# A new first stage for a transformer block: strips first, a second head group's strips, wide q stores, unread products in the waits

## The chip, the cores and the metric

The kernel runs on one core of one Trainium2 chip. The metric is the device time of one execution in microseconds (us). Engine names are those of the profile: PE is TensorE (its matmuls), PEld its weight loads, DVE is VectorE, ACT is ScalarE, POOL is GpSimd, SP is SyncE. SPq and ACTq are the DMA issues of SP and ACT.

## The reference

An adaLN transformer block on x of 8 batches, 512 tokens and 128 channels, cut here to what matters:

```python
mod = (silu(c) @ wmod).reshape(8, 6, 1, 128)       # sa, ca, ga, sb, cb, gb
h = layernorm(x) * (1 + ca) + sa
q, k, v = heads(h @ bin(Wq).T + bq), ...           # 16 heads of 8; bin(W) = sign(W) * mean|W| of a row
x = x + ga * (softmax(q @ k.T * 8**-0.5) @ v @ bin(Wp).T + bp)
h = layernorm(x) * (1 + cb) + sb
x = x + gb * (shared_ffn(h) + top2_of_8_experts(h))
```

## The kernel before

Attention comes first, batch by batch (B0 to B7), then a mixture of experts in units of rows. In attention a batch has 16 slots. A slot n takes one head group (four heads, `n // 4`) and one quarter of the keys: four score products (`scores`, L1609), four exponentials on ACT (L868), and one slot later the products with v (`products`, L1620). An exponential needs the row's maximum. It is found ahead of time in "fills": `max_scores` makes q·k for one head and half of the queries into a bank of 1,024 columns (L1594), and `maxima` reduces it on DVE (L1077). There are 32 fills to a batch, eight to a head group. Steady slots have two fills. Slots 0 to 4 of B0 have three (`CATCH_UP`), as they begin with 11 fills (`FIRST_FILLS`) made ahead of them.

Scores are made of bf16 parts: q and k are split in three (`first_part` on DVE, then `split_qk`), stored to DRAM (`store_q_heads`, the k stores of ACT), and read back as stacks of 72 rows (`load_q_stack`, `load_k_stack`). The stack's last two rows are the negated maxima: after eight fills, `max_T` transposes them, `split_max` splits them on DVE, and a DMA lays them in (`m_row_loaded`). This trip is long, so the fills of B0's head group 0 (`DIRECT_FILLS`, 8) don't use the stacks: `project_direct` (L1646) projects the same heads a second time in f32, each head in a strip of 32 partitions, and `max_scores` multiplies the strips directly (L1584), four matmul instructions a fill. DVE reduces these at L1074.

The first stage is thus, by engine and in program order:

- SP: loads x, the four weights, bq, bk, bv, bp, router bias, three shared matrices, then x of B1 once B0's layer norm is done; stores q's parts in six DMAs (head group 0, then the rest), loads x of B2, then the q stacks of groups 0 and 1, waits for group 1's stack and the row maxima (L523), and loads groups 2 and 3.
- DVE: layer norm of B0, weight cleaning (`clean_weights`, twice), statistics of B1, q's first part and whole split, layer norm of B1, k's first part, fills 0 to 7, `split_max`, fills 8 to 10.
- PE: c and router transposes, modulation, `ln1_T(B0)`, `spread_bias` (biases into the strips; waits for all five small loads), `weights_T(0)`, `project` q, `project_direct` k and q, `project` k, fills 0 to 10 with `weights_T(2)`, `project_v`, `ln1_T(B1)`, `project` q of B1 and `max_T` between them, `project` k of B1, then slot 0.
- ACT: evacuates each of these in PE's order; stores and loads k's parts of groups 0 and 1.
- POOL: constants, reciprocal deviations (`rstd`), k's split.

`misc` is one PSUM bank that all transposes and projections share, in the order of the list `BEFORE`; each waits until the one before is evacuated.

Of the kernel before, what the change touches and what calls it, by code (L numbers as in the profile page):

```python
# [5 lines left out]
ALU = mybir.AluOpType  # L6
# [5 lines left out]
P = 128  # L12
B, T, C = 8, 512, 128
H = 16
DH = C // H
TT = T // P
HG = 4
# [20 lines left out]
DIRECT = 1  # L38
DIRECT_FILLS = DIRECT * 2 * HG
# [14 lines left out]
def adaln_block(nc: bass.Bass, x, Wq, bq, Wk, bk, Wv, bv, Wp, bp, sh_gate, sh_up, sh_down,  # L54
                gate_w, up_w, down_w, router_w, routing_bias, c, wmod, out):
    ctx = ExitStack()
    with ctx:
# [26 lines left out]
        w_sgn = scratch[0][:, 0:4 * C].rearrange("p (i c) -> p i c", c=C)  # L84
        w_neg = scratch[0][:, 4 * C:8 * C].rearrange("p (i c) -> p i c", c=C)
# [128 lines left out]
        first_stored = [sem(f"first_stored{i}") for i in range(2)]  # L214
        small_loaded = sem("small_loaded")
        c_loaded = sem("c_loaded")
# [85 lines left out]
        BEFORE = ["c", "mod", "ln1_0", "q_0", "k_0", "v_0", "ln1_1", "q_1", "m0", "k_1"]  # L302
# [119 lines left out]
        def first_part(dve, b, i, done):  # L422

            if b.const > 0:
                dve.wait_ge((q_stored, k_stored)[i], all_stored(b.plus(-1), i))
            if b.const == 1:
                dve.wait_ge(first_stored[i], 16 * (PARTS, 1)[i])
            dve.wait_ge(misc_free, done + 1)
            dve.tensor_copy(qk_parts[i][:, 0, :], qk_f[i][:]).then_inc(first_ready, 1)  # L429
# [13 lines left out]
        def load_k_stack(eng, b, g):  # L443

            eng.wait_ge(*((first_stored[1], 16) if b.const == 0 and g == 0 else (k_stored, all_stored(b, 1))))
# [37 lines left out]
        def _(sp):  # L483
            sp.dma_start(x_in[:], x[0].rearrange("(p t) c -> p t c", p=P)).then_inc(x_in_loaded, 16)
            for i, w in enumerate((Wq, Wk, Wv, Wp)):
                sp.dma_start(w_nat[:, i, :], w).then_inc(w_loaded[i // 2], 16)
            for i, v in enumerate((bq, bk, bv)):
                sp.dma_start(bias_qkv[:, i:i + 1], v.rearrange("(p o) -> p o", o=1)).then_inc(small_loaded, 16)
# [5 lines left out]

            def load_x(b):

                sp.wait_ge(ln1_ready, TT * b.n)
                sp.dma_start(x_in[:], x[bass.ds(b.n, 1)].rearrange("o (p t) c -> p (o t) c", p=P)).then_inc(x_in_loaded, 16)
# [19 lines left out]
            def load_q_stack(b, g):  # L518
# [3 lines left out]
                if b.const > 0 or g > 0:  # L522
                    sp.wait_ge(q_stored, all_stored(b, 0))  # L523
# [54 lines left out]
            for i in range(2):  # L578
                store_parts(B1, i)
# [94 lines left out]
        def _(pool):  # L674
# [11 lines left out]
            def rstd(mv, ve, ve_ready, out_, ready, stats_ready, b):  # L686
# [8 lines left out]
            pool.affine_select(out=earlier_token[:], in_=ones_bf[:], compare_op=ALU.is_gt, fill=0.0, base=0,  # L695
                               pattern=[[1, P]], channel_multiplier=-1).then_inc(consts_ready, 1)
            pool.memset(marks[:], 0.0).then_inc(consts_ready, 1)

            pool.sem_inc(rows_free, 2)
            pool.iota(expert_no[:], pattern=[[1, E]], base=0, channel_multiplier=0,  # L700
                      allow_small_or_imprecise_dtypes=True).then_inc(consts_ready, 1)
            pool.iota(next_row[0][:], pattern=[[REGION, E]], base=0, channel_multiplier=0,
                      allow_small_or_imprecise_dtypes=True).then_inc(consts_ready, 1)
            for k in range(RING):
                pool.memset(digit[:, k:k + 1], float(E ** k)).then_inc(consts_ready, 1)
            pool.memset(pad_rows[:], 0.0).then_inc(pad_ready, 1)
            pool.wait_ge(pad_ready, 1)
            pool.memset(pad_rows[:, :, C + 1], float(FAR)).then_inc(pad_ready, 1)
            pool.iota(first_row[:], pattern=[[REGION, E]], base=0, channel_multiplier=0,
                      allow_small_or_imprecise_dtypes=True).then_inc(consts_ready, 1)  # L710
            pool.iota(unit_start[:], pattern=[[P, 2 * EARLY_PAIRS]], base=0, channel_multiplier=0,
                      allow_small_or_imprecise_dtypes=True).then_inc(consts_ready, 1)
            pool.affine_select(out=earlier[:], in_=ones_bf[:, 0:E * E].rearrange("p (e f) -> p e f", e=E), compare_op=ALU.is_gt,
                               fill=0.0, base=0, pattern=[[1, E], [-1, E]], channel_multiplier=0).then_inc(consts_ready, 1)
            pool.iota(home[:], pattern=[[TOKENS, K_TOP], [1, TT]], base=0, channel_multiplier=TT,
                      allow_small_or_imprecise_dtypes=True).then_inc(setup_pool, 1)
# [53 lines left out]

            pool.wait_ge(setup_pool, 4)
            rstd(mv1, ve1, var1_ready, rstd1, rstd1_ready, stats1_ready, B1)
            split_qk(pool, B0, 1)
# [51 lines left out]
        def _(act):  # L825
# [91 lines left out]
            for h0, h1, stored in ((0, HG, first_stored[1]), (HG, H, k_stored)):  # L917
                act.dma_start(k_dram[0][h0:h1].rearrange("h d i t -> (h d) i t"), qk_parts[1][DH * h0:DH * h1]).then_inc(stored, 16)
# [102 lines left out]
        def _(dve):  # L1021
# [251 lines left out]

            dve.memset(strip_rows[:], 0.0).then_inc(strips_ready, 1)
# [208 lines left out]
        def _(pe):  # L1483
# [10 lines left out]

            pe.wait_ge(consts_ready, 2)
            pe.wait_ge(c_loaded, 32)
            pe.transpose(misc[:, 0:B], c_nat[:], ident[0:B, 0:B])
            pe.transpose(misc[:, B:B + E], router_nat[:], ident[0:E, 0:E]).then_inc(misc_full, 1)
            free(use(AHEAD, "mod"))
# [72 lines left out]
            def max_scores(b, g, hh, half):  # L1572
# [3 lines left out]
                if fill < DIRECT_FILLS:  # L1576
                    g, pair, t = direct_fill(fill)
                    if fill % (2 * HG) == 0:
                        pe.wait_ge(first_done, (4,)[g])
# [300 lines left out]
```

## Time and profile before

| | |
|---|---|
| median of 3 runs | 668.17 us (664.99 to 668.57) |
| the profiled execution | 667.02 us, its span 665.2 us |
| mean granted TensorE clock | 0.977 |
| PE busy | 615.2 us, 92% |
| DVE busy | 504.9 us, 76% |
| ACT busy | 404.1 us, 61% |

The span runs from the first to the last instruction. Busy shares are averages over stages with different limits. The granted clock is given as a share of 2.4 GHz, so 0.5 is the lower level of 1.2 GHz. The first stage is the first 37 us; slots 0 to 4 of B0 follow, up to 60.6 us.

### The profile page before, as it was taken

To read this page: it belongs to the slowest core of one execution; us is meant where nothing else is said; L and a number is where in the kernel's file an instruction comes from. 1 tells how busy PE (TensorE), PEld (TensorE's weight loads), DVE (VectorE), ACT (ScalarE), POOL (GpSimd) and SP (SyncE) were. 2 spreads that over 40 slices of the span, in tenths; PEclk is the share of its full clock that TensorE was granted. 3 is DMA by queue.
4 is the path that set the end of the run, shared out by engine and by line. 5 is a ranking of instruction groups with operands and counts; after the bars stand their busy time and mean duration, and the time that the engine had idled before them with its cause. 6 is when DMAs were issued, how large, how long until landed. Compare 5 with 4: busy or idle time off the path is not lost.

```text
span 665.2 us, 10688 instructions
## 1 busy us (share of the span) xinstructions
PE 615.2 (92%) x3461; PEld 288.7 (43%) x3461; DVE 504.9 (76%) x1065; ACT 404.1 (61%) x791; POOL 259.2 (39%) x309
## 2 busy tenths in 40 slices
PE   4899999999999999999999999999999589886997
PEld 2332324233333333423333333232378578776855
DVE  5779788889988989888998888988467534433567
ACT  2345777777777776777778778678735224433431
POOL 4240041414352451434336235025056656566610
PEclk9969999999999999999999999999999988997999
DMA  3443332442541445344244244214832223222155
GB/s 103 134 121 117 117 114 98 132 131 90 160 123 64 133 134 134 109 149 116 93 147 127 69 133 130 67 50 135 226 81 57 68 65 88 63 68 61 56 185 195
DMA packets 58828, 73.91 MB, mean 111 GB/s; under 512 B 10857, under 2 KB 39819, under 8 KB 58772
## 3 DMA queue, kind: packets, MB, share of 16 engines
q1 hardware_dynamic: 53144, 63.30, 32.0%
q0 software_dynamic: 4320, 8.47, 3.7%
q10 hardware_dynamic: 1308, 1.46, 0.8%
q8 instruction: 28, 0.46, 0.3%
q14 instruction: 28, 0.23, 0.1%
HBM read 38.36 MB, written 34.96 MB: 110 GB/s over the span
## 4 chain that ended last, share of the span: by engine, by line
PE 73%; DVE 12%; ACT 7%; issue 3%; another core or an unknown queue 2%; DMA 1%; SPq 1%; POOL 1%; ACTq 1%; DVEq 0%; POOLq 0%
PE pv L1620 15%; PE st L1609 15%; PE mx L1594 14%; PE mx L1806 7%; DVE neg_max L1077 6%; PE st L1820 5%; PE mx L1754 3%; PE misc L1487 2%; PE misc L1514 2%; PE st L1770 2%; ACT pt L868 2%; PE pv L1794 1%; PE misc L1520 1%; DVE stats_sb L1026 1%
## 5 line engine op out<-in xcount | busy, mean ns | idle before, releaser
L868 ACT ACTIVATE pt<-st 128x512 f32<-128x512 f32 x496 | 282.1, 598 | 105.8 <-PE st L1609 95.9
L1077 DVE TENSOR_REDUCE neg_max<-mx 128x2 f32<-128x1024 f32 x248 | 294.5, 1215 | 47.9 <-PE mx L1594 44.6
L1620 PE MATMUL pv<-pt,vs 128*32 128x512 f32 x1024 | 136.4, 605 | 0.3 <-ACT pt L868 0.3
L745 POOL DMA_INDIRECT routed<-rec,row_u x64 | 64.1, 1002 | 136.6 <-PE pv L1620 114.8
L812 POOL DMA_INDIRECT results<-qs,home_u x71 | 72.0, 1014 | 50.8 <-ACT qs L995 28.4
L1609 PE MATMUL st<-even_qk 74*128 74x512 bf16 x256 | 89.0, 389 | 1.9 <-ACT pt L868 1.1
L1609 PE MATMUL st<-qs,ks 74*128 74x512 bf16 x240 | 81.4, 383 | 1.8 <-ACT pt L868 1.1
L1594 PE MATMUL mx<-ks,qs 72*128 72x512 bf16 x256 | 76.5, 380 | 2.9 <-DVE neg_max L1077 2.5
L1594 PE MATMUL mx<-even_qk 72*128 72x512 bf16 x240 | 74.5, 393 | 4.4 <-DVE neg_max L1077 4.1
L437 POOL TENSOR_TENSOR qk_r<-qk_f,qk_parts 128x512 f32<-128x512 f32 x15 | 17.4, 1161 | 98.8 <-DVE qk_parts L429 98.7
L1609 PEld LDWEIGHTS st<-even_qk 74*128 74x128 bf16 x256 | 20.9, 99 | 71.5 <-ACT pt L868 51.7
L989 ACT ACTIVATE vs<-mx 128x512 f32<-128x512 f32 (+1 forms) x43 | 22.7, 527 | 43.8 <-PE mx L1806 20.9
L1609 PEld LDWEIGHTS st<-qs,ks 74*128 74x128 bf16 x240 | 18.8, 98 | 67.5 <-ACT pt L868 51.5
L1806 PE MATMUL mx<-vs,pt 128*128 128x256 f32 (+1 forms) x224 | 48.1, 361 | 0.0
L1370 DVE TENSOR_TENSOR vs<-vs,mx 128x512 f32<-128x512 f32 (+1 forms) x29 | 17.2, 591 | 36.8 <-ACT vs L989 34.4
L1620 PEld LDWEIGHTS pv<-pt,vs 128*32 128x32 f32 x1024 | 20.1, 108 | 52.9 <-issue 37.6
L995 ACT ACTIVATE qs<-st,ks 128x128 f32<-128x128 f32 x71 | 23.2, 370 | 32.2 <-PE st L1820 20.6
L1806 PEld LDWEIGHTS mx<-vs,pt 128*128 128x128 f32 x224 | 38.8, 208 | 3.4
L1594 PEld LDWEIGHTS mx<-even_qk 72*128 72x128 bf16 x240 | 22.2, 100 | 35.0 <-DVE neg_max L1077 13.0
L1594 PEld LDWEIGHTS mx<-ks,qs 72*128 72x128 bf16 x256 | 23.7, 98 | 31.4 <-DVE neg_max L1077 8.2
L1794 PE MATMUL pv<-ident,ks 128*128 128x128 f32 x71 | 15.7, 287 | 21.9 <-ACT vs L984 13.4
L1370 DVE TENSOR_TENSOR pt<-vs,mx 128x512 f32<-128x512 f32 (+1 forms) x14 | 8.3, 591 | 24.0 <-issue 23.5
(217 smaller groups left out, 798.0 us busy)
## 6 DMA issues: line engine op xcount, KB each, us to landing
routed<-pad_rows SPq DMA_DIRECT2D x64, 260.0 KB
even_qk<-q_parts SPq DMA_DIRECT2D x48, 96.0 KB
qs<-q_parts SPq DMA_DIRECT2D x48, 96.0 KB
ks<-k_parts SPq DMA_DIRECT2D x48, 96.0 KB
even_qk<-k_parts SPq DMA_DIRECT2D x42, 96.0 KB
ks<-routed SPq DMA_DIRECT2D x28, 130.0 KB
q_parts<-qk_parts SPq DMA_DIRECT2D x21, 128.0 KB
k_parts<-qk_parts SPq DMA_DIRECT2D x7, 384.0 KB, 2.3
```

The costliest lines, as they stand in the source:

```text
L745: pool.indirect_dma_start(out=routed_dram, out_offset=bass.IndirectOffsetOnAxis(ap=row_u[:, k, t:t + 1], axis=0), in_=rec[b.par][:, k, t, ...
L812: pool.indirect_dma_start(out=result_dram, out_offset=bass.IndirectOffsetOnAxis(ap=home_u[:, slot, h:h + 1], axis=0), in_=y_u[slot][:, h, ...
L868: act.activation(pt[n % 2][:, hh, :], score_bank(b, n, hh), ACT.Exp, scale=SCALE).then_inc(exp_done, 1)
L989: act.activation(silu_u[u % 2][:, 0:halves(u) * I], up_bank(u, 0), ACT.Silu).then_inc(silu_ready, 1)
L995: last = act.activation(y_u[u % RING][:, h, :], y_bank(u)[:, h, :], ACT.Copy, scale=xu[u % RING][:, h, C:C + 1])
L1077: dve.tensor_reduce(neg_max[g % 2][:, hh, 2 * half:2 * half + 2], mx_bank[half][:], AX_X, ALU.max, negate=True).then_inc(mx_free, 1)
L1370: dve.tensor_tensor(act_u[u % ARING][:, 0:halves(u) * I], silu_u[u % 2][:, 0:halves(u) * I], up_bank(u, 1), ALU.mult).then_inc(act_ready, 1)
L1594: last = pe.matmul(mx_bank[half][:, t, :], qs[b.par][0:PROD, h, q0:q0 + P], ks[b.par][0:PROD, h, :], start=True, stop=True)
L1609: pe.matmul(score_bank(b, n, hh), ks[b.par][0:STACK, h, j * P:(j + 1) * P], qs[b.par][0:STACK, h, :], start=True, stop=True).then_inc(st_f ...
L1620: last = pe.matmul(pv_bank[32 * hh:32 * (hh + 1), :], vs[b.par][:, j, HG * g + hh, :], pt[n % 2][:, hh, :], start=(n % Y_SLOTS == 0), stop ...
L1806: last = pe.matmul(up_bank(u, m // IC)[:, m % IC * rows:(m % IC + 1) * rows], w_unit[u % WRING][:, m * P:(m + 1) * P], xuT[u % 2][:, 0:row ...
L1820: last = pe.matmul(y_bank(u)[:, h, :], act_u[u % ARING][:, first:first + P], w_unit[u % WRING][:, 2 * I + j * C:2 * I + (j + 1) * C], star ...
```

## The change

The strips of head group 1 are made too, and the fills that use strips become twelve (all of the 11 made ahead, and the first of slot 0). Strips are projected ahead of q itself. `spread_bias` waits for bq and bk alone, which are loaded right after Wq and Wk. q's parts are split on POOL, stored in three DMAs of all heads, and the stacks are loaded group by group. `max_T` of group 0 comes ahead of `ln1_T(B1)`. `keep_busy` puts matmuls into PE's waits whose products nobody reads: bf16, 128x128 by 128x512, into a free bank. In all there are 33 of them: 7, 5, 4, 2 and 2 ahead of the first projection, 1, 1, 1, 1, 4 and 1 between the fills, and 3 ahead of slot 0; and a DVE memset makes their operand.

```diff
-DIRECT = 1
-DIRECT_FILLS = DIRECT * 2 * HG
+DIRECT = 2
+DIRECT_FILLS = 3 * HG
...
-        BEFORE = ["c", "mod", "ln1_0", "q_0", "k_0", "v_0", "ln1_1", "q_1", "m0", "k_1"]
+        BEFORE = ["c", "mod", "ln1_0", "q_0", "k_0", "v_0", "m0", "ln1_1", "q_1", "k_1"]
...
@@ sync
-            for i, w in enumerate((Wq, Wk, Wv, Wp)):
-                sp.dma_start(w_nat[:, i, :], w).then_inc(w_loaded[i // 2], 16)
-            for i, v in enumerate((bq, bk, bv)):
-                sp.dma_start(bias_qkv[:, i:i + 1], v.rearrange("(p o) -> p o", o=1)).then_inc(small_loaded, 16)
+            for i, w in enumerate((Wq, Wk)):
+                sp.dma_start(w_nat[:, i, :], w).then_inc(w_loaded[0], 16)
+            for i, v in enumerate((bq, bk)):
+                sp.dma_start(bias_qkv[:, i:i + 1], v.rearrange("(p o) -> p o", o=1)).then_inc(qk_bias_loaded, 16)
+            for i, w in enumerate((Wv, Wp)):
+                sp.dma_start(w_nat[:, 2 + i, :], w).then_inc(w_loaded[1], 16)
...
+            load_x(B1)
+            sp.dma_start(bias_qkv[:, 2:3], bv.rearrange("(p o) -> p o", o=1)).then_inc(small_loaded, 16)
...
-            load_x(B1)
             sp.wait_ge(parts_ready, 1)
-            store_q_heads(0, HG, first_stored[0])
-            store_q_heads(HG, H, q_stored)
-            load_x(B1.plus(1))
-            sp.wait_ge(first_stored[0], 16 * PARTS)
+            store_q_heads(0, H, q_stored)
             load_q_stack(B0, 0)
-            load_q_stack(B0, 1)
-            sp.wait_ge(stack_loaded[0][1], STACK_DMAS)
-            sp.wait_ge(m_row_loaded[0], ROW_DMAS)
-            for g in (2, 3):
+            for g in (1, 2, 3):
                 load_stack(B0, g)
+                if g == 2:
+                    load_x(B1.plus(1))
...
@@ gpsimd
+            split_qk(pool, B0, 0)
+            split_qk(pool, B0, 1)
+            rstd(mv1, ve1, var1_ready, rstd1, rstd1_ready, stats1_ready, B1)
             pool.affine_select(out=earlier_token[:], in_=ones_bf[:], compare_op=ALU.is_gt, fill=0.0, base=0,
...
             pool.wait_ge(setup_pool, 4)
-            rstd(mv1, ve1, var1_ready, rstd1, rstd1_ready, stats1_ready, B1)
-            split_qk(pool, B0, 1)
             fill_values(pool, 1)
...
@@ scalar
-            act.wait_ge(setup_pool, 3)
-            for i in range(2):
-                load_ones(act, i)
...
             evacuate_wT(0, 2)
-            act.wait_ge(small_loaded, 80)
-            evacuate_qk(B0, 0, use(AHEAD, "q_0"))
             act.wait_ge(first_done, 1)
             evacuate_direct(1, 0, 3)
             evacuate_direct(0, 0, 4)
+            evacuate_qk(B0, 0, use(AHEAD, "q_0"))
             evacuate_qk(B0, 1, use(AHEAD, "k_0"))
+            act.wait_ge(setup_pool, 3)
+            load_ones(act, 0)
             evacuate_wT(2, 5)
             act.activation(exp_first[:], strip_rows[:], ACT.Exp)
-            act.wait_ge(parts_ready, 2)
...
             act.wait_ge(v_ready[0], 2)
             evacuate_v(B0, use(AHEAD, "v_0"))
+            act.wait_ge(parts_ready, 2)
+            for h0, h1, stored in ((0, HG, first_stored), (HG, H, k_stored)):
+                act.dma_start(k_dram[0][h0:h1].rearrange("h d i t -> (h d) i t"), qk_parts[1][DH * h0:DH * h1]).then_inc(stored, 16)
+            evacuate_direct(1, 1, 6)
+            evacuate_direct(0, 1, 7)
             act.wait_ge(key_ones[0], 16)
             load_k_stack(act, B0, 0)
-            load_k_stack(act, B0, 1)
-            project_in(B1, use(AHEAD, "ln1_1"))
-            evacuate_qk(B1, 0, use(AHEAD, "q_1"))
+            act.wait_ge(small_loaded, 48)
             act.wait_ge(misc_free, use(AHEAD, "m0") + 1)
             for k in range(M_PARTS):
                 act.dma_start(qs[0][MROW + k:MROW + k + 1, 0:HG, :].rearrange("p h (t q) -> p (h t) q", t=TT),
                               m_rows[0][:, k, :]).then_inc(m_row_loaded[0], 16)
+            project_in(B1, use(AHEAD, "ln1_1"))
+            evacuate_qk(B1, 0, use(AHEAD, "q_1"))
+            load_ones(act, 1)
...
@@ vector
             first_part(dve, B0, 0, use(AHEAD, "q_0"))
-            split_qk(dve, B0, 0)
+            maxima(range(1))
+            first_part(dve, B0, 1, use(AHEAD, "k_0"))
+
+            maxima(range(1, 2 * HG))
             layer_norm1(B1)
-            first_part(dve, B0, 1, use(AHEAD, "k_0"))
-
-            maxima(range(DIRECT_FILLS))
             split_max(B0, 0, use(AHEAD, "m0"))
-            maxima(range(DIRECT_FILLS, FIRST_FILLS))
+            maxima(range(2 * HG, FIRST_FILLS))
...
@@ tensor
+            def keep_busy(count, into):
+
+                ones = busy_ops.bitcast(BF16)
+                for _ in range(count):
+                    pe.matmul(into, ones[:, 0:P], ones, start=True, stop=True)
...
-                pe.wait_ge(small_loaded, 80)
+                pe.wait_ge(qk_bias_loaded, 32)
...
+            keep_busy(4, nothing)
             ln1_T(B0, use(AHEAD, "ln1_0"))
             spread_bias()
+            keep_busy(2, nothing)
             weights_T(0)
-            pe.wait_ge(first_done, 2)
+            keep_busy(2, nothing)
+            free(use(AHEAD, "q_0"))
+            project_direct(1, 0, 2)
+            project_direct(0, 0, 2)
             project(0, use(AHEAD, "q_0"))
-            project_direct(1, 0, 1)
-            project_direct(0, 0, 2)
-            project(1, use(AHEAD, "k_0"))
...
             for fill in range(FIRST_FILLS):
                 max_scores(*fill_of(fill))
+                if fill == 0:
+                    project(1, use(AHEAD, "k_0"))
                 if fill == 1:
+                    keep_busy(1, pv_bank[:])
                     weights_T(2)
+                if fill == 2:
+                    keep_busy(1, pv_bank[:])
                 if fill == 3:
                     pe.wait_ge(first_done, 5)
                     project_v(use(AHEAD, "v_0"))
+                if fill == 4:
+                    keep_busy(1, st_bank[0][:])
                 if fill == 5:
+                    project_direct(1, 1, 4)
+                    project_direct(0, 1, 4)
+                if fill == 6:
+                    keep_busy(1, st_bank[0][:])
+                if fill == 2 * HG - 1:
+                    keep_busy(4, st_bank[0][:])
+                    max_T(B0, 0, use(AHEAD, "m0"))
+                if fill == 2 * HG:
                     ln1_T(B1, use(AHEAD, "ln1_1"))
-                if fill == DIRECT_FILLS - 1:
+                if fill == 2 * HG + 1:
+                    keep_busy(1, st_bank[0][:])
                     project(0, use(AHEAD, "q_1"))
-                    max_T(B0, 0, use(AHEAD, "m0"))
             project(1, use(AHEAD, "k_1"))
+            keep_busy(3, st_bank[0][:])
```

## Rows read from the trace of the kernel before

**Rows 1.** The page: span, and granted clock in 40 slices (tenths).

```profile
span 665.2 us, 10688 instructions
...
PEclk9969999999999999999999999999999988997999
```

**Rows 2.** The chain of waits by time: start us, us, what.

```profile
7.59 2.81 DMA router_bias<-L_ffn_routing_bias
...
60.51 3.40 DVE neg_max L1077 x3
...
72.69 0.86 PE misc L1514 x2
73.77 0.43 PE mx L1594 x2
```

**Rows 3.** Stretches: us, then busy of PE, PEld, DVE, ACT, POOL; clock; DMA share; GB/s.

```profile
10.00:15.00 5.00, 4.08 (x20) 1.39 (x24) 2.80 (x15) 1.49 (x4) 0.58 (x2) 1.00 0.38 115
...
35.00:40.00 5.00, 5.00 (x11) 1.72 (x10) 2.81 (x3) 1.88 (x4) 0.00 (x0) 0.50 0.28 80
...
66.00:200.00 134.00, 130.99 (x747) 45.97 (x746) 115.64 (x197) 100.22 (x183) 42.64 (x50) 1.00 0.40 120
```

**Rows 4.** Single microseconds: the same columns, around the clock's fall.

```profile
29.00:30.00 1.00, 0.00 (x0) 0.00 (x0) 1.00 (x2) 0.68 (x1) 0.00 (x0) 1.00 0.71 206
...
31.00:32.00 1.00, 0.38 (x1) 0.00 (x0) 0.00 (x0) 0.58 (x1) 0.00 (x0) 0.52 0.23 58
```

**Rows 5.** Timeline, up to 18 us: start us, us, engine, line, instructions [idle before].

```profile
6.37 1.68 DVE L1034 TENSOR_SCALAR ln<-x_in,mv,rstd 128x128 f32<-128x128 f32 x4 [1.58 <-POOL rstd L691]
...
8.19 1.09 PE L1487 MATMUL misc<-ident,ln 128*128 128x128 f32 x4 [1.11 <-DVE ln L1034]
...
9.24 0.48 DVE L1052 TENSOR_SCALAR w_nat<-pt,alpha 128x128 f32<-128x128 f32 x2
...
9.38 0.78 ACT L845 ACTIVATE hT<-misc,mod_T 128x512 f32<-128x512 f32 x1 [2.02 <-PE misc L1487]
...
10.66 0.69 PE L1628 MATMUL st<-ident,w_nat 128*128 128x128 f32 x2
...
11.39 0.38 ACT L893 ACTIVATE wT<-st 128x256 f32<-128x256 f32 x1 [0.33 <-PE st L1628]
...
13.83 1.94 PE L1646 MATMUL st<-hT,wT 128*32 128x512 f32 x8
...
14.00 0.69 ACT L853 ACTIVATE qk_f<-misc,bias_qkv 128x512 f32<-128x512 f32 x1 [2.23 <-PE misc L1514]
```

**Rows 6.** Timeline from 18 us to slot 0: the same columns.

```profile
18.46 1.99 PE L1584 MATMUL mx<-x 32*128 32x512 f32 x8
...
19.63 4.81 DVE L1074 TENSOR_REDUCE neg_max<-mx 128x2 f32<-128x1024 f32 x4
19.79 1.15 POOL L437 TENSOR_TENSOR qk_r<-qk_f,qk_parts 128x512 f32<-128x512 f32 x1 [4.10 <-DVE qk_parts L429]
...
25.69 3.58 ACTq L448 DMA_DIRECT2D even_qk<-k_parts  x6
...
33.20 1.24 ACTq L928 DMA_DIRECT2D even_qk<-m_rows  x2
```

**Rows 7.** Timeline from slot 0 on: the same columns.

```profile
37.40 1.06 PE L1609 MATMUL st<-even_qk 74*128 74x512 bf16 x2
...
39.35 1.22 DVE L1077 TENSOR_REDUCE neg_max<-mx 128x2 f32<-128x1024 f32 x1 [2.19 <-PE mx L1594]
...
45.10 1.22 DVE L1077 TENSOR_REDUCE neg_max<-mx 128x2 f32<-128x1024 f32 x1 [1.59 <-PE mx L1594]
...
51.34 1.07 PE L1620 MATMUL pv<-pt,vs 128*32 128x512 f32 x8
...
69.25 0.60 PE L1487 MATMUL misc<-ident,ln 128*128 128x128 f32 x4
```

**Rows 8.** DMA issues by line: KB each, us from issue to landing.

```profile
k_parts<-qk_parts ACTq DMA_DIRECT2D x1, 96.0 KB, 2.6
```

More of the change, by code:

```diff
@@ L84, in adaln_block @@
         w_sgn = scratch[0][:, 0:4 * C].rearrange("p (i c) -> p i c", c=C)
+        busy_ops = scratch[1][:, 0:T // 2]
         w_neg = scratch[0][:, 4 * C:8 * C].rearrange("p (i c) -> p i c", c=C)
@@ L213, in adaln_block @@
         strips_ready = sem("strips_ready")
-        first_stored = [sem(f"first_stored{i}") for i in range(2)]
+        busy_ready = sem("busy_ready")
+        first_stored = sem("first_stored")
         small_loaded = sem("small_loaded")
+        qk_bias_loaded = sem("qk_bias_loaded")
         c_loaded = sem("c_loaded")
@@ L425, in first_part @@
                 dve.wait_ge((q_stored, k_stored)[i], all_stored(b.plus(-1), i))
-            if b.const == 1:
-                dve.wait_ge(first_stored[i], 16 * (PARTS, 1)[i])
+            if b.const == 1 and i == 1:
+                dve.wait_ge(first_stored, 16)
             dve.wait_ge(misc_free, done + 1)
@@ L443, in load_k_stack @@
         def load_k_stack(eng, b, g):
-            eng.wait_ge(*((first_stored[1], 16) if b.const == 0 and g == 0 else (k_stored, all_stored(b, 1))))
+            eng.wait_ge(*((first_stored, 16) if b.const == 0 and g == 0 else (k_stored, all_stored(b, 1))))
             for j in range(PARTS):
@@ L694, in _ @@
             rstd(mv1, ve1, var1_ready, rstd1, rstd1_ready, stats1_ready, B0)
[L695 to L716, printed above, removed]
             def residual(b):
@@ L769, in scatter @@
                     scatter_rows(b, i)
+            split_qk(pool, B0, 0)
+            split_qk(pool, B0, 1)
+            rstd(mv1, ve1, var1_ready, rstd1, rstd1_ready, stats1_ready, B1)
+            pool.affine_select(out=earlier_token[:], in_=ones_bf[:], compare_op=ALU.is_gt, fill=0.0, base=0,
+                               pattern=[[1, P]], channel_multiplier=-1).then_inc(consts_ready, 1)
+            pool.memset(marks[:], 0.0).then_inc(consts_ready, 1)
+            pool.sem_inc(rows_free, 2)
+            pool.iota(expert_no[:], pattern=[[1, E]], base=0, channel_multiplier=0,
+                      allow_small_or_imprecise_dtypes=True).then_inc(consts_ready, 1)
+            pool.iota(next_row[0][:], pattern=[[REGION, E]], base=0, channel_multiplier=0,
+                      allow_small_or_imprecise_dtypes=True).then_inc(consts_ready, 1)
+            for k in range(RING):
+                pool.memset(digit[:, k:k + 1], float(E ** k)).then_inc(consts_ready, 1)
+            pool.memset(pad_rows[:], 0.0).then_inc(pad_ready, 1)
+            pool.wait_ge(pad_ready, 1)
+            pool.memset(pad_rows[:, :, C + 1], float(FAR)).then_inc(pad_ready, 1)
+            pool.iota(first_row[:], pattern=[[REGION, E]], base=0, channel_multiplier=0,
+                      allow_small_or_imprecise_dtypes=True).then_inc(consts_ready, 1)
+            pool.iota(unit_start[:], pattern=[[P, 2 * EARLY_PAIRS]], base=0, channel_multiplier=0,
+                      allow_small_or_imprecise_dtypes=True).then_inc(consts_ready, 1)
+            pool.affine_select(out=earlier[:], in_=ones_bf[:, 0:E * E].rearrange("p (e f) -> p e f", e=E), compare_op=ALU.is_gt,
+                               fill=0.0, base=0, pattern=[[1, E], [-1, E]], channel_multiplier=0).then_inc(consts_ready, 1)
+            pool.iota(home[:], pattern=[[TOKENS, K_TOP], [1, TT]], base=0, channel_multiplier=TT,
+                      allow_small_or_imprecise_dtypes=True).then_inc(setup_pool, 1)
             pool.wait_ge(setup_pool, 4)
-            rstd(mv1, ve1, var1_ready, rstd1, rstd1_ready, stats1_ready, B1)
-            split_qk(pool, B0, 1)
             fill_values(pool, 1)
@@ L1272, in late_tables @@
                     unit_experts(EARLY_PAIRS, TABLE - EARLY_PAIRS, tables_ready)
+            dve.memset(busy_ops, 1.0).then_inc(busy_ready, 1)
             dve.memset(strip_rows[:], 0.0).then_inc(strips_ready, 1)
@@ L1492, in free @@
                 pe.wait_ge(misc_free, done)
+            def keep_busy(count, into):
+                ones = busy_ops.bitcast(BF16)
+                for _ in range(count):
+                    pe.matmul(into, ones[:, 0:P], ones, start=True, stop=True)
+            nothing = mx_bank[1][:, 1, :]
+            pe.wait_ge(busy_ready, 1)
+            keep_busy(7, nothing)
             pe.wait_ge(consts_ready, 2)
@@ L1498, in _ @@
             pe.transpose(misc[:, B:B + E], router_nat[:], ident[0:E, 0:E]).then_inc(misc_full, 1)
+            keep_busy(5, nothing)
             free(use(AHEAD, "mod"))
@@ L1587, in max_scores @@
                     return
-                if hh == 0 and half == 0:
+                if hh == 0 and half == 0 or fill == DIRECT_FILLS:
                     pe.wait_ge(stack_loaded[b.par][g], STACK_DMAS * (b.half + 1))
```

13 lines of the change are left out of this document (5 added, 8 removed).

## The prediction

> **What bounds the kernel now.** I read the page first. Its span is 665.2 us, and of the 40 slices the third is the only one of the attention part in which PE's granted clock is clearly down [rows 1]. The windows come next, as they say what bounds each stage: from 66 to 200 us PE is busy 131 of 134 us, DVE 116, ACT 100 [rows 3]. So attention from slot 6 on is bound by PE, and the change touches nothing there. What the change can give is a shift: the time at which the first slots of B0 are done. I look for one event that fixes it and take the end of fill 26, the last of three reductions that the chain of waits shows from 60.51 to 63.91 [rows 2]. From there to 200 us the program is the same and its order too.
>
> Before that event there are three stretches. Up to 18.5 us the strips and projections are made. In this stretch the windows print a clock of 1.00 [rows 3], but the durations contradict it: eight instructions of strip projection take 1.94 us, and the same shape takes 1.07 at 51.34 [rows 5, 7]. I take it that PE ran at its lower level and that the record has no entry until the clock changes. From 18.5 to 37.4 DVE and PE take turns, DVE reduces fills 0 to 7 in some 10.6 us from 19.63 [rows 6], then everything waits for stacks and row maxima. The clock is recorded as falling to the lower level at 31 us, behind a microsecond with no PE work [rows 4], and is still there at 40 [rows 3]. From 37.4 on slots 0 to 4 run, and there DVE decides: three reductions to a slot at 1.13 to 1.2 us each [rows 2], with idle time of 2.19 and 1.59 ahead of fills 11 and 14 [rows 7].
>
> **The change, part by part.** Full-level prices: 0.86 us for a projection, 0.43 for two bf16 products of 512 columns, so 0.215 for one [rows 2]; 1.0 for four strip projections (1.07 as busy time [rows 7]); 0.95 for a strip fill, half of 1.99 for eight instructions [rows 6]; 0.60 for four transposes [rows 7]. A reduction takes 1.21 [rows 6].
>
> *Start to fill 0.* B0's layer norm ends at 8.05 as before [rows 5]; nothing of the change is ahead of it but a memset on DVE and the order of loads behind x. If the first 16 unread products have brought the clock up, transposes take 0.60 for 1.09, and hT (0.78) is ready near 9.55. `spread_bias` no longer waits for the router bias, which landed at 10.4 [rows 2]. The cleaned weights are there at 9.72 [rows 5], their transposes and copy (0.69 halved, 0.38) end near 10.5, and the two pairs of unread products (4 x 0.215) fit into the waits. The first projection starts at 10.5, not 11.8 (the copy ends at 11.77 [rows 5]). k strips, q strips and q follow: 1.0 + 1.0 + 0.86, to 13.35. ACT copies the q strips by 13.35, fill 0 starts at 13.4 for 18.46 [rows 6]. ACT then has q at 14.1 (0.69 [rows 5]), DVE its first part at 14.6, and reduces fill 0 from there: 5.0 us ahead of 19.63 [rows 6].
>
> *Fills 0 to 7.* PE now has more to do here: project k after fill 0, the strips of group 1 after fill 5 (2.0 us), eight unread products. DVE does k's first part (0.43), but no split. Followed in order, with a fill waiting for the reduction two before it: reductions of fills 1, 2, 3 run back to back from 16.5 to 20.1; fill 4 is late behind `project_v` (as many columns as a projection, 0.86) by 0.6; fill 6 is late behind the strips by 1.8 (PE 21.9 to 23.9, then the fill to 24.8). The last reduction ends at 27.3. That is 12.7 us for eight fills, where before it was 10.6, and gives back 2.1 of the 5.0.
>
> *To slot 0.* Before, nothing reduced from 30.2 to 33.6, as fill 8 needed group 1's stack and DVE waited for `max_T`. Now `max_T` runs at 27.4 (its four unread products, 0.86, end at 26.8 and cost nothing), B1's layer norm takes DVE to 28.4, `split_max` to 28.95. ACT issues the row maxima to 30.2 (1.24 [rows 6]), which puts hT of B1 behind them, to 31.0. PE: fill 8, transposes of B1, fill 9 and one unread product by 30.6, a wait of 0.45, project q to 31.9, fill 10 to 32.85, project k to 33.7 (ACT frees the bank at 32.7), three unread products to 34.35. Here the 0.64 us are on the path, as nothing waits there: I book them in full. Slot 0 starts at 34.35 for 37.4 [rows 7], 3.0 earlier.
>
> *Slots 0 to 4.* Fill 11 is now a strip fill: 0.95 for 0.43, so its reduction starts near 35.85, for 39.35 [rows 7]: 3.5 earlier. From there the DVE work is unchanged. Before it took 63.91 - 39.35 = 24.56 us, of which 1.59 ahead of fill 14 was waiting for PE at the lower level [rows 7]. With PE at its upper level this wait goes, but some 0.5 remains, as PE alternates with DVE in slots 2 and 3. Gain there 1.1. The sum at fill 26 is 3.5 + 1.1 = 4.6 us.
>
> *Transfers.* q's split moves from DVE to POOL, three steps of which the first is 1.15 [rows 6]; I take 3.2 us: parts at 17.8, k's at 21.0, as POOL does one after the other. q's store waits for all heads: three issues to 20, landing after 2.6 to 4 us, by 24 at the latest (the row is of 96 KB [rows 8]). k's store by ACT ends with its first group landed at 24.1 (2.6 [rows 8]), behind it stand the copies of the new strips (to 24.7), then three loads of 0.6 each (3.58 for six [rows 6]), to 26.6. Landed by 29.5 if they take 3 us. Slot 0 needs them at 34.35: 4.8 us of cover. Groups 1 to 3 are loaded by SP from 24 on at about 3.7 us each; group 1 is needed only by fill 12, no longer by fill 8. B2's x moves behind group 2 and is needed in slot 1. POOL's constants move behind the splits and feed nothing before slot 0 except the v values of B1, which end near 27. All of these I cost at nothing, with that cover.
>
> *Where a page speaks against it.* Rows 3 and 5 show a recorded 1.00 beside matmuls at half speed. The Trainium skill ("TensorE: Matmul & The Clock Gate", Part 1) says that the lower clock is the default and that activity lifts it; by this rule the trace agrees. The same page (Part 4) says that transposes don't count as activity, which would leave the first rise to the unread products alone. If the rise comes in the first 8 us, the sum stays; if not, it is the first rival.
>
> **Sum.** 667.0 for the profiled execution less 4.6 is 662.4; the same off the median of 668.2 is 663.6. I forecast 663.0. A difference under 0.5% (3.3 us) can't be told from none.
>
> **The rivals.** *The clock is late.* The rises in the trace came only behind long full-width work (13.83 on), and with a gap between the first seven and the next five products it may stay low until after the first projections. Then what I took at full level is at half: 16 unread products take 3.4 us more, of which about 1 stands ahead of `ln1_T` (it would start near 9.1); transposes, weights and four more products add 0.5, 0.35 and 0.4 on the path. The first projection would start near 12.8. Gain 4.6 - 2.3 = 2.3, time 665. For it: nobody can see the clock's phase. Chance 0.14.
>
> *The clock falls all the same before slot 0.* Strip fills use 64 rows, they are most of the work, and before it fell at 31 after them. If it falls near 31, q, fill 10, k and three products take 3.35 more, fill 11 0.95 more, and the 1.1 of slots 0 to 4 is lost: 4.6 - 5.4, time 667.5. Against it: in my walk PE waits at most 0.5 at a time there, where before it had a whole microsecond without work at 29 [rows 4]. Chance 0.1.
>
> *Slower.* It is the same fall, but earlier, behind the strips of group 1 at 24. Then fills 6 to 10 take 0.95 more each (4.75), the projections 1.7, the unread products 1.9, transposes 0.5, fill 11 0.95; less the waits they fill (some 1.5), 8.3 us. It decides from the point at which slot 0 starts later than about 41 (37.4 and 3.3 us more). Slot 0 would start near 41.7 (34.35, and 8.3 less the 0.95 of fill 11), and with the 1.1 lost too the sum is 4.6 - 8.3 - 1.1, 4.8 us later than before: 672. The chance is 0.06: before, 18.5 to 29 held the upper level on just such fills [rows 6].
>
> *The stacks are late.* Slot 0's start is then the landing of k's group 0. It takes 4.8 us more than I think to show, and 8 to lose all. Time 663 to 668, chance 0.05.
>
> *More gain.* The waits of DVE ahead of fills 4 and 6 (0.6 + 1.8) come out half as long, and the 1.59 of slots 0 to 4 is recovered whole: 1.2 + 0.5 on top of 4.6, 6.3 us, time 661 off the profiled execution. Chance 0.12. The forecast itself, 661 to 664.7, keeps 0.53.
>
> **Numbers.** Faster by over 0.5% (under 664.8): forecast, more gain, and less than half of the late clock and late stacks, 0.71. Within 0.5%: the rest of these and the fall at 31, 0.21. Slower: 0.08. The range runs from 659 to 667.6, leaving the slower rival and single runs as far apart as those of before (665.0 to 668.6) outside.
>
> **What would show it.** In the profile after: strip projections of 1.0 to 1.1 us near 10.5; first reduction at L1074 near 14.6, the eighth ending near 27.3; DVE idle of about 1.8 ahead of fill 6; twelve, not eight, reductions at L1074; first scores near 34.4; no 0.5 in the third slice; end of fill 26 near 59.3. The prediction is wrong if PE's clock is at 0.5 between 24 and 45 us, if the first scores wait for a DMA, or if fill 26 is early and the end isn't, which would put the loss behind 60 us.

## The result, and the profile after

Over 20 executions each, the changed kernel takes 665.81 us (663.47 to 667.73) and the one before 668.08 (664.99 to 670.88): ratio 0.9967, interval 0.9953 to 0.9981. It is faster, by 2.3 us, where I had forecast 663.0 and a gain of 4.6 of the profiled execution's 667.0. The time lies in the range that I gave (659 to 667.6), but the gain is less than half of the forecast: 2.3 us of 4.6, or of the 5.1 from 668.08 to 663.0. At 0.33% it is also under the 0.5% that I had drawn as the line to "none", an outcome to which I gave a chance of 0.21 against 0.71 for more. On another chip the changed kernel (run a1) has a ratio of 0.9973 (0.9952 to 0.9994). The ratios leave out executions more than 1.5% above the fastest of their kernel: one in e1, one in e2 and two in e8.

The profiled execution of the changed kernel took 667.73 us, by chance the slowest of its 20, so its span says nothing of the gain. I read the stages instead. The page first, against [rows 1]:

```profile
span 666.0 us, 10815 instructions
...
PEclk9999999999999999999999999999999899998899
```

The third slice is at 9, not 6: the fall of the clock ahead of slot 0 is gone. The chain of waits by time (start us, us, what):

```profile
10.31 1.07 PE st L1661 x8
11.38 0.86 PE pv L1661 x8
12.23 1.06 PE misc L1529 x2
13.29 1.06 PE mx L1599 x4
14.35 1.06 PE misc L1529 x2
15.40 1.06 PE mx L1599 x4
...
17.00 1.06 PE mx L1599 x4
18.06 0.32 PE pv L1504
18.38 1.06 PE mx L1599 x4
19.44 1.09 PE misc L1535 x8
20.53 1.06 PE mx L1599 x4
21.58 0.32 PE st L1504
21.91 1.06 PE mx L1599 x4
22.96 0.99 PE st L1661 x8
23.96 0.86 PE pv L1661 x8
24.82 1.06 PE mx L1599 x4
...
26.20 1.08 PE mx L1599 x4
...
27.30 1.23 DVE neg_max L1078
28.53 1.02 DVE ln L1038 x4
...
29.77 0.29 DVE m_rows L1091
...
57.32 3.40 DVE neg_max L1081 x3
...
69.50 0.86 PE misc L1529 x2
70.58 0.44 PE mx L1609 x2
```

Two things are to be seen. Fill 26 ends at 60.72, for 63.91 [rows 2], 3.2 us earlier and not 4.6; the projection 72.69 in [rows 2] is now at 69.50, the same 3.2. And from 10.31 to 27.28 every piece but 0.16 us ahead of `weights_T(2)` is PE's, without a wait for DVE: the stage is bound by PE, strip fills (`mx`, x4) cost 1.06 each, and so do the projections (`misc`, x2) that stand between them. The pieces of 0.32 are single unread products. The windows of the same stretches as in [rows 3], and one of 134 us beginning 3 us earlier (columns as there):

```profile
10.00:15.00 5.00, 4.87 (x25) 1.39 (x24) 2.92 (x13) 2.41 (x4) 0.45 (x1) 1.00 0.39 93
...
35.00:40.00 5.00, 4.64 (x21) 1.83 (x20) 3.03 (x5) 2.97 (x5) 0.51 (x1) 1.00 0.70 157
63.00:197.00 134.00, 130.78 (x746) 45.99 (x746) 115.64 (x197) 100.19 (x182) 42.68 (x50) 1.00 0.39 120
```

The last is the same work in the same time as before (130.78 for 130.99 of PE). The rows of the timeline that answer to [rows 5 to 7]:

```profile
7.69 0.63 PE L1492 MATMUL misc<-ident,ln 128*128 128x128 f32 x4 [0.26 <-DVE ln L1038]
...
10.31 1.07 PE L1661 MATMUL st<-hT,wT 128*32 128x512 f32 x8
...
14.39 1.23 DVE L1078 TENSOR_REDUCE neg_max<-mx 128x2 f32<-128x1024 f32 x1
...
25.92 1.23 DVE L1078 TENSOR_REDUCE neg_max<-mx 128x2 f32<-128x1024 f32 x1 [1.69 <-PE mx L1599]
...
30.13 1.41 ACTq L929 DMA_DIRECT2D even_qk<-m_rows  x2
...
36.14 0.60 PE L1624 MATMUL st<-even_qk 74*128 74x512 bf16 x2
...
37.84 1.23 DVE L1078 TENSOR_REDUCE neg_max<-mx 128x2 f32<-128x1024 f32 x1 [1.97 <-PE mx L1599]
```

Transposes take 0.63 where they took 1.09, and the first strips 1.07 where they took 1.94: the clock is up before the first transposes at 7.69. The very first unread products, from 1.25 on, still took 3.17 us for seven; the four from 6.40 on took 1.02. Of DMA issues, k's part of head group 0 landed in:

```profile
k_parts<-qk_parts ACTq DMA_DIRECT2D x1, 96.0 KB, 1.8
```

**A landmark.** Single executions of one kernel lie some 5 us apart, so experiments on 1 us need a finer measure. In each profile I take the start of the first copy of a finished half batch to `y_strips` on ACT, in slot 8 of B0 where PE bounds already. The rows give the group of all 16 copies, first and last start. Before, then after:

```profile
L874 ACT ACTIVATE y_strips<-pv x16: 597/597/598, 75.5 to 478.4; 128x512 f32<-128x512 f32 x16
```

```profile
L874 ACT ACTIVATE y_strips<-pv x16: 597/598/600, 72.3 to 475.4; 128x512 f32<-128x512 f32 x16
```

The lead of 3.2 is still 3.0 at the end of attention. The rest, a mixture-of-experts part that the change doesn't touch, took 665.2 - 478.4 = 186.8 in the one profile and 666.0 - 475.4 = 190.6 in the other. Three further profiles with total times near these (b3, b4 and a2 below) have 188.7, 188.4 and 188.6. Thus what the pair of spans seems to lose there is that part's own scatter.

### The profile page after: what moved, and what is told of

It is laid out like the page before. It is cut to its first block, busy times and chain, and to the rows that moved or that the text cites. A ratio compares the mean times of both kernels' runs of the same rounds, so it can differ in the third digit from the quotient of the medians.

```text
span 666.0 us, 10815 instructions
## 1 busy us (share of the span) xinstructions
PE 619.9 (93%) x3523; PEld 289.2 (43%) x3525; DVE 502.2 (75%) x1063; ACT 406.2 (61%) x793; POOL 262.6 (39%) x312
## 4 chain that ended last, share of the span: by engine, by line
PE 71%; DVE 13%; ACT 7%; another core or an unknown queue 4%; issue 3%; DMA 1%; POOL 1%; ACTq 0%; DVEq 0%; POOLq 0%
PE pv L1635 15%; PE st L1624 14%; PE mx L1609 13%; PE mx L1839 7%; DVE neg_max L1081 6%; PE st L1853 4%; PE mx L1787 3%; PE misc L1492 2%; PE misc L1529 2%; PE st L1803 2%; ACT pt L868 2%; PE mx L1599 2%; DVE ln L1038 1%; PE misc L1535 1%
## 5 line engine op out<-in xcount | busy, mean ns | idle before, releaser
L1081 DVE TENSOR_REDUCE neg_max<-mx 128x2 f32<-128x1024 f32 x244 | 289.6, 1216 | 43.6 <-PE mx L1609 40.3
L815 POOL DMA_INDIRECT results<-qs,home_u x71 | 72.1, 1016 | 54.1 <-ACT qs L999 36.8
L1624 PE MATMUL st<-even_qk 74*128 74x512 bf16 x256 | 87.6, 383 | 2.4 <-ACT pt L868 1.5
L1609 PE MATMUL mx<-even_qk 72*128 72x512 bf16 x232 | 69.4, 380 | 4.0 <-DVE neg_max L1081 3.4
L1839 PE MATMUL mx<-vs,pt 128*128 128x256 f32 (+1 forms) x224 | 49.9, 371 | 0.0
```

The costliest lines, as they stand in the source:

```text
L815: pool.indirect_dma_start(out=result_dram, out_offset=bass.IndirectOffsetOnAxis(ap=home_u[:, slot, h:h + 1], axis=0), in_=y_u[slot][:, h, ...
L1081: dve.tensor_reduce(neg_max[g % 2][:, hh, 2 * half:2 * half + 2], mx_bank[half][:], AX_X, ALU.max, negate=True).then_inc(mx_free, 1)
L1609: last = pe.matmul(mx_bank[half][:, t, :], qs[b.par][0:PROD, h, q0:q0 + P], ks[b.par][0:PROD, h, :], start=True, stop=True)
L1624: pe.matmul(score_bank(b, n, hh), ks[b.par][0:STACK, h, j * P:(j + 1) * P], qs[b.par][0:STACK, h, :], start=True, stop=True).then_inc(st_f ...
L1839: last = pe.matmul(up_bank(u, m // IC)[:, m % IC * rows:(m % IC + 1) * rows], w_unit[u % WRING][:, m * P:(m + 1) * P], xuT[u % 2][:, 0:row ...
```

## The experiments

The runs were made on four chips. On three of them (e1 to e9, a1, b1, b2) the part behind attention takes some 25 us less, 641.0 to 641.7 us in all for the kernel before; on the fourth (b3, b4, a2, e10) that kernel takes 668.15 us, as in the result. So only ratios and landmarks go from one to the other. "Before" has landmarks 75.5, 73.2, 75.4, 74.2, 74.4 in five profiles; "changed" has 72.3, 71.9, 72.2.

A count first: the diff has 32 unread products, not 33 (20 ahead of the first projection, 9 between the fills, 3 ahead of slot 0). So e2 takes out 12 and not the 13 that its expectation names, and without the seven of e10 25 are left, not 26.

**e1: no unread products.**

```diff
-                for _ in range(count):
+                for _ in range(0):
                     pe.matmul(into, ones[:, 0:P], ones, start=True, stop=True)
```

> The changed kernel with all 33 unread products taken out (they feed nothing, so the result is the same). I read the traces by a landmark, the start of the first copy into y_strips (75.5 us before, 72.3 after), as it scatters less than the whole time. Theory A, the unread products mostly cost PE time in a stage that PE bounds, and the clock doesn't need them: the landmark at 72 to 73. Theory B, they hold the clock: it comes up only near 17 us and falls again near 31, and the landmark is at 75 or later, most or all of the gain gone.

Ratio to before 1.007 (1.0043 to 1.0096), landmark 79.0, and slower than before by more than the change gains. (Six executions.) Theory A falls. The first strips, which took 1.07, are again at the lower level, and the clock is at 0.5 from 31 to 48 us. Only its rise came sooner than theory B had it: at 14.02 a projection already takes 1.12, not at 17. The timeline and the windows (PE busy, clock, DMA share, GB/s):

```profile
10.51 1.93 PE L1661 MATMUL st<-hT,wT 128*32 128x512 f32 x8 [0.57 <-ACT wT L893]
```

```profile
28.00:30.00 2.00, 0.60 (x3) 1.00 0.79 154
30.00:32.00 2.00, 1.90 (x10) 0.74 0.79 154
```

The new order without the unread products has the f32 strip fills 9 to 11 in the slow stretch, at 2.08 each, where before had bf16 ones; it is worse off than the old.

**e2: the first 20 kept, the 12 from fill 1 on taken out.**

```diff
-                    keep_busy(1, pv_bank[:])
                     weights_T(2)
...
-                    keep_busy(4, st_bank[0][:])
                     max_T(B0, 0, use(AHEAD, "m0"))
...
-            keep_busy(3, st_bank[0][:])
```

> The changed kernel with the first 20 unread products kept and the 13 from fill 1 on taken out. Theory A (what is on PE's path costs 0.22 us each): three ahead of slot 0 and about two between the fills are saved, the landmark moves from 72.3 to 71.2 to 71.7, the clock stays up. Theory B (the clock falls without them, near 31 us): strip fills and projections behind it take twice as long, landmark 74 to 75.5.

Ratio 1.0052 (1.0033 to 1.0072), landmark 76.9: theory B, and more than it expected. The windows (PE, PEld, DVE, ACT, POOL, clock, DMA):

```profile
26.00:28.00 2.00, 0.65 (x3) 0.39 (x5) 2.00 (x6) 0.00 (x0) 0.28 (x3) 1.00 0.81 191
28.00:30.00 2.00, 1.89 (x10) 0.89 (x8) 1.91 (x4) 0.00 (x0) 0.00 (x0) 0.69 0.78 179
30.00:32.00 2.00, 2.00 (x5) 0.50 (x6) 0.05 (x1) 0.78 (x1) 0.00 (x0) 0.50 0.84 200
```

The clock falls behind a stretch in which PE had 0.65 us of work in 2, the wait for DVE's eighth reduction. A strip fill then takes 2.01 in the chain of this run.

**e3: strips for head group 0 alone; e5: the same with 14 unread products ahead of fill 8.**

```diff
-DIRECT = 2
-DIRECT_FILLS = 3 * HG
+DIRECT = 1
+DIRECT_FILLS = 2 * HG
...
-                    project_direct(1, 1, 4)
-                    project_direct(0, 1, 4)
```

```diff
                     max_T(B0, 0, use(AHEAD, "m0"))
+                    keep_busy(14, st_bank[0][:])
```

> The changed kernel with strips for head group 0 alone, so fills 8 to 11 go by the stacks as before. Theory A, that the second group's strips are the term I undersized: 2.0 us of projections after fill 5 and 0.6 us more per fill for four fills go, the landmark moves to 70.5 to 71.8. Rival, the stack of group 1 is late for fill 8 (its last k load is issued at 28.3 us in the trace after): fill 8 starts at 30.5 to 31.5 and not at 28.9, and the landmark is 72.3 to 73.5, so the second group is worth its price.

> The changed kernel with strips for head group 0 alone and 14 more unread products (3.0 us) in the wait ahead of fill 8. The kernel with one group's strips had its landmark at 75.3 us, with the clock at 0.5 from 29 to 40 us. If the second group's strips gain because fill 8 needs no stack, this one stays behind: 74 or more. If they gain only because they keep PE at work in that wait, this one is level with the changed kernel: 72 to 73, and the clock stays at 1.0.

e3: ratio 1.0004 (0.9985 to 1.0023), landmark 75.3, later than both theories had it. Fill 8 starts at 32.07, later than the rival said, and the clock falls in the wait (0.70 in the microsecond from 28, then 0.50). The timeline:

```profile
32.07 1.03 PE L1607 MATMUL mx<-even_qk 72*128 72x512 bf16 x2 [4.92 <-DMA even_qk<-k_parts]
```

e5: the clock stays at 1.0 and the landmark is 72.6, so in the profiles most of what the second group's strips give, 2.7 of 3.2 us (75.3 to 72.6 and to 72.1), is that they fill this wait. But its ratio is 1.0009 (0.9986 to 1.0031), 12 executions between 639.2 and 643.4, where the changed kernel has 0.9973 and one of 12 above 640.05. Two things in the record bear on it. In the profile fill 8 still waits for group 1's stack:

```profile
31.59 0.61 PE L1607 MATMUL mx<-even_qk 72*128 72x512 bf16 x2 [1.42 <-DMA even_qk<-k_parts]
```

And the seven executions with a mean clock of 0.999 or 1.0 have a median of 640.4, while the other five, at 0.994 to 0.997, hold the four slowest (642.4 to 643.4). So the clock probably still falls in some executions, perhaps when the stack lands late; none of those was profiled.

**e4 and e8: the kernel before with unread products.** e4 has the first 20 at the changed kernel's places. e8 adds the early loads of bq and bk, single products behind fills 1, 2, 4 and 6, and groups from fill 7 on:

```diff
                 if fill == DIRECT_FILLS - 1:
+                    keep_busy(5, st_bank[0][:])
                     project(0, use(AHEAD, "q_1"))
+                    keep_busy(3, st_bank[0][:])
                     max_T(B0, 0, use(AHEAD, "m0"))
+                    keep_busy(4, st_bank[0][:])
             project(1, use(AHEAD, "k_1"))
+            keep_busy(3, st_bank[0][:])
```

> The kernel before with the first 20 unread products added at the same places, nothing else changed. Theory A, the early clock rise alone: first projections at 1.1 us instead of 1.9, the k parts 2 to 2.5 us earlier, group 1's stack and fill 8 as much earlier, landmark 73 to 73.5 if the later fall at 31 us stays as it was. Rival, the whole gain of the change is this rise and the absent fall: landmark at 72.5 or less. Second rival, bias load at 10.4 us and the stack transfers hold the stage: landmark 75 or more.

> The kernel before with what the change does to the clock and the first waits alone: bq and bk loaded early, the 20 first unread products, single ones behind fills 1, 2, 4, 6, and 5, 3, 4 and 3 of them in the waits from fill 7 to slot 0. Strips of one head group, order of projections, splits and stores as before. If the clock is the main part of the gain, the clock stays at 1.0 and the landmark is at 71.5 to 73. If the new order and the second group's strips are the main part, the landmark is at 73.5 or later though the clock stays up.

e4: ratio 1.0005 (0.9982 to 1.0028), 640.4 to 648.7; the profiled one is the slowest, landmark 80.7, with the clock at 0.5 from 12 to 15 and from 22 to 49 us. There PE waited from 8.7 to 11.9 for the router bias. The second rival had that wait and a landmark of 75 or more, but none of the three expectations had the clock: in this execution it was up early, and fell early too, behind the wait that was left.

e8: the profile has the clock at 1.0 throughout and the earliest landmark but one, 70.4, earlier than the 71.5 to 73 expected. But its 12 executions make two groups, five at 637.7 to 638.5 with a mean clock of 1.0, and seven at 645.4 to 647.9 with 0.983 to 0.987; ratio 1.0022 (0.9982 to 1.0063) without its two slowest, and over all twelve a median of 645.62 for 641.04. With the clock held, the old order and one group's strips are 1.7 us ahead of the changed kernel's landmark (mean 72.1), though fill 0 starts at 14.55 and not at 13.22. So the new order isn't what gains time by itself. What e8 lacks is a held clock in more than half of its executions. Where the clock falls in those I didn't see.

**e6, e7, e10: fewer unread products.** e6 drops the single ones behind fills 1, 2, 4 and 6, e7 the three ahead of slot 0, e10 all seven.

```diff
                 if fill == 1:
-                    keep_busy(1, pv_bank[:])
                     weights_T(2)
-                if fill == 2:
-                    keep_busy(1, pv_bank[:])
...
             project(1, use(AHEAD, "k_1"))
-            keep_busy(3, st_bank[0][:])
```

> The changed kernel without the four single unread products behind fills 1, 2, 4 and 6; the groups of 4, 1 and 3 behind them stay. In the trace after each of these four takes some 0.3 us of a stretch in which PE is busy without a pause. Theory A (they only cost, the others hold the clock): the landmark moves from 72.1 to 71.0 to 71.6. Theory B (strip fills alone let the clock fall): it falls between 24 and 32 us, landmark 74 or more, time 0.5% over the changed kernel's.

> The changed kernel without the three unread products ahead of slot 0, 0.65 us on the chain that ended last. If they are needed for nothing, the landmark moves from 72.1 to 71.4 to 71.7 and the clock stays up. Rival: the clock falls at the start of slot 0, landmark 73 or more. Third: slots 0 to 4 wait on DVE anyway and the landmark stays.

> The changed kernel without the four single unread products behind fills 1, 2, 4 and 6 and without the three ahead of slot 0. Alone, the four gave 1 us (landmark 71.0) and the three 0.2 to 0.5 (71.7). If what holds the clock are the other 26, the landmark is at 70.4 to 70.8. Rival: with all seven gone the clock falls in some executions, which shows as single times 4 us or more above the rest with a clock under 0.995.

e6: ratio 0.9954 (0.9937 to 0.9970), landmark 71.0. e7: 0.9963 (0.9948 to 0.9978), landmark 71.7. e10, on the chip of b3, b4 and a2: 0.9925 (0.9903 to 0.9947), 662.86 us for 668.15, landmark 70.3; its mean clocks, 0.982 to 0.990, are those of the changed kernel on that chip (0.979 to 0.990), and no execution stands apart from the rest. The seven products only cost; the other 25 hold the clock (20 alone, in e2, did not). e10 beats both kernels. In e6 strip fills stand back to back again, and the timeline shows what that does:

```profile
20.03 1.99 PE L1599 MATMUL mx<-x 32*128 32x512 f32 x8
...
25.95 0.81 PE L1504 MATMUL st<-pt 128*128 128x512 bf16 x3 [0.16 <-issue]
27.48 0.27 PE L1542 MATMUL misc<-ident,neg_max 128*16 128x128 f32 x1 [0.72 <-DVE neg_max L1078]
```

Two fills take 1.99 (1.92 in the chain), where two apart take 1.06 each. And the wait for DVE ahead of `max_T`, in which e2 lost the clock, is here filled with the four products for somewhat more than half (0.81 us seen of them, then 0.72 idle).

**e9: q stored in six DMAs again.**

```diff
-            store_q_heads(0, H, q_stored)
+            store_q_heads(0, HG, first_q)
+            store_q_heads(HG, H, q_stored)
```

> The changed kernel with q stored in six DMAs, the first head group ahead, instead of three wide ones. By my prediction's transfers, which I costed at nothing behind 4.8 us of cover, the landmark stays at 72 to 72.4. Rival: SP issues three more DMAs of 0.75 us ahead of the stack loads, group 0's or the later stacks are late, landmark 73 or more.

Landmark 72.0, ratio 0.9974 (0.9952 to 0.9995), as the changed kernel. The wide stores do nothing here.

**a1, a2 and b1 to b4: both kernels again, unaltered.**

> The changed kernel again, unaltered, on the chip and beside the kernels of this call. If the gain is made in the first stage and is the same on every chip, its landmark (start of the first copy into y_strips) is again at 72 to 72.6 us and the time 2 to 3 us under that of before. If part of the gain exists only against executions of before in which the clock falls in the first stage, the time is 0 to 2 us under that of before.

> The kernel before, unaltered, for a second profile. Theory C: the fall of the clock at 31 us in the first profile is a matter of the execution; without it the landmark is at 72.5 to 73.5 us, not 75.5, and the mean granted clock is above 0.99. Rival: it falls in every execution, landmark 75 to 76.

> The kernel before, unaltered, for a third profile. As for the second: by theory C some of these profiles show no fall and a landmark of 72.5 to 73.5 us, by its rival all show 75 to 76.

> The kernel before, unaltered, a fourth profile. So far its landmark was at 75.5, 73.2 and 75.4 us, with a fall of the clock between 29 and 31 in all three. If the profile that I predicted from was an ordinary one, this and the next are at 75 to 76; if the phase of the clock moves it, they lie anywhere from 73 to 76.

> The kernel before, unaltered, a fifth profile. As for the fourth: 75 to 76 if the first profile was ordinary, anywhere from 73 to 76 if the phase of the clock moves the landmark.

> The changed kernel, unaltered, a third profile. As it never lost the upper level in the first stage, its landmark should scatter little: 71.8 to 72.4, as 72.3 and 71.9.

a1 and a2: landmarks 71.9 and 72.2. The kernel before lost the clock in all five profiles, so theory C falls in its strong form, but the fall costs more in one execution than in another. The windows of b1 (PE busy, clock, DMA share, GB/s) have it at 0.5 from 28.2 to 38.4 us; in the first profile, whose row stands last, it was there from 31 [rows 4] to 44.7:

```profile
28.00:30.00 2.00, 1.02 (x2) 0.55 0.75 182
...
38.00:40.00 2.00, 1.57 (x6) 0.89 0.51 148
```

```profile
44.00:45.00 1.00, 1.00 (x5) 0.65 0.52 163
```

And the chain of b1 at fills 24 to 26:

```profile
58.21 3.40 DVE neg_max L1077 x3
```

Against 60.51 [rows 2], 2.3 us earlier in the same program. Over the five profiles the landmark follows the time at which the clock came back: 38.4, 39.5, 42.8, 43.9 and 44.7 us by single-microsecond windows (b1, b3, b4, b2, the first), for landmarks of 73.2, 74.2, 74.4, 75.4 and 75.5. The five landmarks of before have a mean of 74.5, the three of after 72.1: a difference of 2.4 us, for 2.27 measured by the time in the result and 1.89 beside a1.

## Why the gain was less than half of the forecast

**The place of the gain and the clock held; the sizes did not.** The gain is made in the first stage, with the clock held and a start of fill 0 that is 5 us earlier (13.2 for 18.46), and the rest of the kernel keeps it. e8 shows that these 5 us are mostly not the new order's: with the early biases and the clock the old order starts fill 0 at 14.55. The step "start to fill 0" came out within 0.2 us: strips at 10.3 (forecast 10.5), the first reduction at 14.39 (14.6).

**The step that failed is "fills 0 to 7".** I took 0.95 for a strip fill, half of a pair that ran back to back [rows 6], and 0.86 for projections from a stretch without strips [rows 2]. In the new order each fill stands alone and costs 1.06, and a projection or `project_v` among them 1.06 to 1.09. A single unread product takes 0.32 there (at 18.06 and 21.58 in the chain), not 0.215. With that PE is the bound from 10.3 to 27.3, where I had DVE running back to back through fills 1 to 3. The eighth reduction ends at 28.53 for 27.3: 1.2 us late. Part of this the singles make themselves: without them (e6) strip fills stand in pairs again at 0.96 each, and the landmark is 1.1 us earlier.

**To slot 0** the same prices cost again: `split_max` ends at 30.05 (28.95), the row maxima are issued by 31.54 (30.2), project q, fill 10 and project k take 3.2 (2.65), and slot 0 starts at 36.1 (34.35). Fill 11's reduction starts at 37.84, 1.5 earlier than before instead of 3.5. **Slots 0 to 4** gave more than forecast: 60.72 - 37.84 = 22.9 for 24.56, 1.7 instead of 1.1. The sum is 1.5 + 1.7 = 3.2 for 4.6: the prices of PE work took 2.0, slots 0 to 4 gave back 0.6, and 1.4 of the missing 2.3 are thus explained.

**The rest, about 0.9 us, is the baseline.** The profile that I subtracted from has its landmark at 75.5 against a mean of 74.5, 1.0 later. I read a fall of the clock as if it had a fixed length, though I wrote of its phase for the kernel after. b1 to b4 show the scatter, and that it goes with the end of the fall. With a gain that is only known to lie between 1.3 and 3.1 us (the interval of the ratio), the split into 1.4 and 0.9 is no finer than that.

**The rivals.** A late clock and a fall ahead of slot 0 didn't happen in any of the three profiles of the changed kernel; e1 and e2 show what such falls cost when the products are taken away, 6.9 and 4.8 us in the landmark (79.0 and 76.9 for 72.1), so the threat was real. That the measured gain of 2.3 us is the one that I gave for the late clock is luck: the clock was not late. (In the rival of the fall my own terms, 4.6 - 5.4, give 667.8 and not 667.5.) Of the three signs by which I would have called the prediction wrong, a clock at 0.5 and a wait of the first scores for a DMA didn't show. The third, fill 26 early and the end not, does stand in the two profiled spans (665.2 and 666.0), but not in the medians of 20 executions. The rule that activity lifts the default lower clock (the Trainium skill, "TensorE: Matmul & The Clock Gate", Part 1) fits e1 against the changed kernel: 1.93 and 1.07 for the same strips. Late stacks didn't happen: in the chain from 10.31 to slot 0 no piece is the landing of a DMA, and e9 moved nothing. But the last three products, which I booked in full with 0.64 us, gave 0.2 to 0.6 in e7 (71.7 for 71.9 to 72.3).

**What stays open**: in which wait e8 loses the clock in seven of twelve executions, and whether e5's time lags its landmark for the same reason. No run takes the early biases, POOL's split of q or the new place of `max_T` alone, so their single shares are not known.

## What to carry to other kernels

Price a matmul in the order in which it will stand: a strip fill cost 0.96 in a pair and 1.06 alone, a projection 0.86 among its like and 1.06 among strips. Before subtracting from a profile whose clock falls, take a few more profiles: the same fall cost between 0 and 2.3 us more here. Unread products are worth their time in waits: the other 25 held the clock, the seven on the path could go, and taking those seven out raised the gain, by the ratio from 0.33% to 0.75% (0.9967 and 0.9925), by the landmark from 2.4 to 4.2 us. And look at single times and their mean clocks, not at one profile: e8's profile is among the best here, and seven of its twelve executions lose the clock.

## What the runs showed of the hardware that I had not expected

A higher clock early can be lost early. With 20 unread products at the start and a wait of 3.2 us behind them (e4), the clock was up by 8 us (transposes in 0.63), fell at 12, came back at 15 and fell again at 22, six to nine microseconds before it does in the kernel before (28.2 to 31), among strip fills, with PE paused for only 0.52 us just before; the landmark was 80.7 instead of 74.5. This is the slowest of e4's twelve executions, 648.65 us; over all of them e4 is level with the kernel before (1.0005). Its windows (PE busy, clock, DMA share, GB/s):

```profile
20.00:22.00 2.00, 1.48 (x9) 1.00 0.16 45
22.00:24.00 2.00, 2.00 (x8) 0.51 0.35 102
24.00:26.00 2.00, 2.00 (x8) 0.50 0.76 224
```

And the lower level outlasts the wait behind which it came. In e1 it held from 31 to 48 us, with PE busy for 16.00 of the 16 us from 32 on, some 6 us of them strip fills:

```profile
36.00:38.00 2.00, 2.00 (x5) 0.50 0.86 127
...
44.00:46.00 2.00, 2.00 (x8) 0.50 0.01 4
```
